# Residual x plus attention moved from VectorE in the attention steps to GpSimd in the dense layer (one core)

## The chip, the cores and the metric

One NeuronCore of a Trainium2 chip runs the whole program in one launch. The metric is device time in microseconds; the figure for the kernel before is the median of three runs. The granted TensorE clock is 0.99 of full speed on average in the profiled execution.

## The reference

Input x and context ctx are both (8, 512, 2048). Per batch and per channel, a correlation over the 512 positions picks 12 shifts, and a weighted sum of shifted context rows is the attention output. A layer norm, a dense layer with eight small gated experts, and a second residual follow.

```python
def _autocorrelation(Q, K, V):            # called with layernorm(x), ctx, ctx
    corr = ifft(fft(q) * conj(fft(k))).real
    w, idx = top_k(corr, 12); w = softmax(w)
    out = sum(w[i] * take_along_axis(v, min(idx[i] + pos, L - 1)))
x = x + tanh(g_xattn[0]) * _autocorrelation(_layernorm(x), ctx, ctx)
base = layernorm(x) @ W_base.T + b_base
gate = softmax(xf @ W_gate.T); thr = sigmoid(xf @ W_thr + b_thr) * 0.125
w = relu(gate - thr) / sum; moe = einsum(h, w, B_w) * 2.0
x = x + tanh(g_ffn[0]) * (base + moe)
```

## The kernel before

**Attention.** 32 steps, one for each batch and chunk of 512 channels (`STEPS`). Transforms are matmuls against tables. Every engine runs its own `step(i, par, phase)`, with the front of chunk i and the back of chunk i-1 in one step. TensorE does `q_spectra(i)` (L422), `turn_w(i-1)` (transposes, L435), `w_spectra(i-1)` (L454, L460), `correlate(i)` (L472), `v_spectra(i+1)` and `out_tiles(i-1)` (L488), which leaves in PSUM, for each half h of a mirrored pair, a cosine part and a sine part. The eight PSUM banks are two sets of four, `X(par)`; `turn_w` may write the banks of a half only once its output has been taken out.

A row of a chunk's output and its mirror image are cosine plus sine and cosine minus sine. VectorE's `residual` (L758, L764), last in its step, forms both: it adds gate times cosine to x rows, then plus or minus gate times sine, in `xres_mem`. SyncE (the DMA queue SP) brings x in for it with ten DMAs per step (`load_res`, L308 and L311) and writes the sum with ten (`store`, L318 and L321) to the scratch `x2`. The x rows lie in mirrored order, so eight of each ten DMAs cover 16 partitions. GpSimd does the folds and the sums of products; its `fold_v` (L834) waits for VectorE's `w_made`.

**Weights.** Then `turn_weights` transposes 20 jobs through PSUM (L1070): `b_w`, sixteen row blocks of `w_base`, `a_w`, the gate and the first normalised row tile. ScalarE takes out the high half (`weights_hi`, L1138) and VectorE the low half (`weights_lo`, L1194). The first four rows of `w_base` are loaded in the last attention steps (`early_weights`), the others by L999 as slots come free.

**Dense layer.** 32 row tiles of 128 rows. For tile i TensorE does `base(i)`, 192 matmuls (L1097), `turn_hw(i)` (L1105), `logits(i+1)` and `experts(i)`, 12 matmuls (L1112 to L1114). ScalarE's step is `gating(i)`, `normalise(i+2)`, `rounded(i+2)` (L1156), `hw_hi(i)` (L1175); VectorE's is `gating(i)`, `statistics(i+2)` (L1202), `hw_lo(i)` (L1249), `finish(i)` (L1256). `experts(i)` waits for `hw_hi(i)` and `hw_lo(i)`, so these stand behind the normalising of tile i+2 in both queues. GpSimd adds the bias to the residual row (L1285) and makes the f16 remainder of the normalised tile (L1281). SyncE issues, in a step: two transposing DMAs of tile i+1 (L1026), the load of tile i+2 into `norm` (L1018), the load of residual row i+1 into one of two `row` buffers (L1032), the store of row i (L1043).

## Time and profile before

| | us |
|---|---|
| median of 3 runs (lowest, highest) | 3028.21 (3028.15, 3030.24) |
| the profiled execution: its own time | 3031.29 |
| its span in the trace | 3029.5 |
| TensorE matmul busy | 2921.9 (96%) |
| VectorE busy | 1606.0 (53%) |
| ScalarE busy | 1012.6 (33%) |
| GpSimd busy | 1454.0 (48%) |
| attention: to the last output matmul | 0 to 1441.8 |
| weights: to the first dense matmul | 1441.8 to 1507.3 |
| dense layer: 32 tiles | 1507.3 to 3029.5 |

Busy shares over the whole span mix the two long stages, of which each has its own limits: VectorE and GpSimd are nearly full in the first and nearly idle in the second. TensorE is nearly full in both.

### The profile page before, as it was taken

The numbers are of one execution on the slowest core, as the hardware profiler recorded it, in microseconds if no ns is written. First come the engines' busy times: TensorE is split into PE (matmuls) and PEld (weight loads), VectorE is DVE, ScalarE is ACT, GpSimd is POOL, SyncE is SP. The second block draws the span as 40 slices with busy tenths as digits, with TensorE's granted clock in tenths as the row PEclk, the third lists the DMA queues.
The fourth block names the chain that finished last, engine by engine and source line by source line (L and its number), as shares of the span: only waits on it lengthen the run. The fifth ranks groups of instructions, "written<-read, shape, count | busy, mean of one in ns | idle before, by whom it ended". The sixth has DMA issues, their size and how long they took to land.

```text
span 3029.5 us, 37059 instructions
## 1 busy us (share of the span) xinstructions
PE 2921.9 (96%) x13184; PEld 1466.0 (48%) x13184; DVE 1606.0 (53%) x2738; ACT 1012.6 (33%) x1672; POOL 1454.0 (48%) x577
## 2 busy tenths in 40 slices
PE   4999999999999999997799999999999999999999
PEld 2445554555545554553644444444444444444444
DVE  3899989999999999998722121121211112111111
ACT  4555556555555545441511121111211112111110
POOL 4788888889888888884031211212112121221210
PEclk8999999999999999999899999999999999999999
DMA  8455544555455554423634132331323313233230
GB/s 201 124 123 126 139 110 118 127 132 125 115 122 125 135 117 102 101 73 111 237 98 111 56 111 75 91 111 55 111 72 94 106 60 111 69 97 99 68 97 28
DMA packets 260355, 324.49 MB, mean 107 GB/s; under 512 B 162911, under 2 KB 163487, under 8 KB 245541
## 3 DMA queue, kind: packets, MB, share of 16 engines
q1 hardware_dynamic: 259922, 323.38, 40.1%
q8 instruction: 29, 0.48, 0.1%
q14 instruction: 56, 0.46, 0.0%
q10 hardware_dynamic: 348, 0.18, 0.0%
HBM read 223.76 MB, written 67.21 MB: 96 GB/s over the span
## 4 chain that ended last, share of the span: by engine, by line
PE 84%; DVE 5%; POOL 3%; issue 2%; DMA 2%; ACT 1%; SPq 1%; ACTq 0%; DVEq 0%; POOLq 0%
PE bank L1097 43%; PE bank L488 7%; PE bank L422 7%; PE bank L454 6%; PE bank L472 5%; PE bank L460 3%; POOL spec_o L869 3%; DVE rows_mem L1256 2%; PE bank L1086 1%; PE bank L1087 1%; PE bank L1088 1%; ACT wt L548 1%; PE bank L435 1%; PE bank L405 1%; PE bank L411 1%
## 5 line engine op out<-in xcount | busy, mean ns | idle before, releaser
L1281 POOL TENSOR_TENSOR rows_mem<-norm,rows_mem 128x2048 f16<-128x2048 f32 x31 | 126.1, 4068 | 1220.7 <-ACT rows_mem L1156 1220.7
L1097 PE MATMUL bank<-w_hi,rows_mem 128*128 128x512 f16 x2048 | 489.3, 379 | 3.8 <-DVE rows_mem L1256 3.8
L1097 PE MATMUL bank<-w_hi,xres_mem 128*128 128x512 f16 x2048 | 489.0, 379 | 3.5 <-DVE rows_mem L1256 3.5
L869 POOL TENSOR_TENSOR spec_o<-spec_o,term 128x1024 f32<-128x1024 f32 x190 | 443.3, 2362 | 40.6 <-DVE term L686 40.6
L1249 DVE TENSOR_TENSOR hwt_lo<-bank,hwt_hi 128x128 f16<-128x128 f32 x32 | 9.3, 292 | 790.4 <-ACT hwt_hi L1175 790.4
L1097 PEld LDWEIGHTS bank<-w_hi,rows_mem 128*128 128x128 f16 x2048 | 200.2, 98 | 251.6 <-DVE rows_mem L1256 13.6
L1097 PEld LDWEIGHTS bank<-w_hi,xres_mem 128*128 128x128 f16 x2048 | 200.2, 98 | 250.6 <-DVE rows_mem L1256 12.7
L488 PE MATMUL bank<-spec_o,table 128*128 128x512 f32 x512 | 249.1, 617 | 19.9 <-POOL spec_o L869 15.8
L1097 PE MATMUL bank<-w_lo,xres_mem 128*128 128x512 f16 x1024 | 262.8, 379 | 0.0
L1097 PE MATMUL bank<-w_lo,rows_mem 128*128 128x512 f16 x1024 | 262.8, 379 | 0.0
L422 PE MATMUL bank<-rows_mem,table 128*128 128x512 f32 x512 | 227.7, 598 | 18.0 <-POOL rows_mem L849 15.7
L454 PE MATMUL bank<-wt,table 128*128 128x512 f16 x1024 | 232.7, 379 | 8.3 <-ACT wt L548 8.3
L472 PE MATMUL bank<-table,prod_a 128*128 128x256 f32 x1024 | 231.5, 385 | 7.2 <-POOL prod_a L855 7.2
L1202 DVE BATCH_NORM_STATS2 stats<-norm 128x6 f32<-128x512 f32 x128 | 79.1, 681 | 299.4 <-DMA norm<-x_scratch 299.4
L1175 ACT ACTIVATE hwt_hi<-bank 128x128 f16<-128x128 f32 x32 | 8.9, 277 | 657.4 <-PE bank L1105 657.4
L472 PEld LDWEIGHTS bank<-table,prod_a 128*128 128x128 f32 x1024 | 193.7, 192 | 43.2 <-POOL prod_a L855 8.0
L422 PEld LDWEIGHTS bank<-rows_mem,table 128*128 128x128 f32 x512 | 98.1, 192 | 142.7 <-issue 142.7
L454 PEld LDWEIGHTS bank<-wt,table 128*128 128x128 f16 x1024 | 97.0, 98 | 130.5 <-ACT wt L548 12.3
L1285 POOL TENSOR_TENSOR rows_mem<-rows_mem,b_rows 128x2048 f32<-128x2048 f32 x32 | 144.1, 4503 | 30.6 <-DMA rows_mem<-x_scratch 30.6
L1097 PEld LDWEIGHTS bank<-w_lo,xres_mem 128*128 128x128 f16 x1024 | 100.2, 98 | 119.1
L1097 PEld LDWEIGHTS bank<-w_lo,rows_mem 128*128 128x128 f16 x1024 | 100.1, 98 | 119.0
L488 PEld LDWEIGHTS bank<-spec_o,table 128*128 128x128 f32 x512 | 92.2, 192 | 130.3 <-issue 102.6
(182 smaller groups left out, 4876.3 us busy)
## 6 DMA issues: line engine op xcount, KB each, us to landing
rows_mem<-in_x_dram SPq DMA_DIRECT2D x32, 1024.0 KB, 13.0
norm<-x_scratch SPq DMA_DIRECT2D x32, 1024.0 KB, 5.5
rows_mem<-x_scratch SPq DMA_DIRECT2D x32, 1024.0 KB, 7.0
out_dram<-rows_mem SPq DMA_DIRECT2D x32, 1024.0 KB, 4.4
norm<-in_x_dram SPq DMA_DIRECT2D x28, 1024.0 KB, 10.8
rows_mem<-in_ctx_dram SPq DMA_DIRECT2D x256, 64.0 KB
rows_mem<-in_ctx_dram SPq DMA_DIRECT2D x64, 256.0 KB
xres_mem<-in_x_dram SPq DMA_DIRECT2D x256, 64.0 KB
```

What stands on the lines that cost most here:

```text
L405: pe.matmul(imag[:, 0, :], v_tab[:, EI, :], v_sym[:, 3, :], start=True, stop=True)
L422: mm = pe.matmul(pair(four, half)[:, row, :], q_tab[:, 2 * half + row, j, :], qf[:, 2 * row + j, :], start=(j == 0), stop=(j == 1))
L454: pe.matmul(pair(to, half)[:, row, :], w_tab[:, h, 2 * half + row, j, :], wt16[:, 0, 2 * y + j, :], start=(j == 0 and h == 0), stop=False)
L460: mm = pe.matmul(pair(to, half)[:, row, :], w_tab[:, 0, 2 * half + row, j, :], wt16[:, 1, 2 * y + j, :], start=False, stop=(j == 1))
L472: mm = pe.matmul(four[:, ct, row * HALF:(row + 1) * HALF], prod_a[:, slot, ct * 128:(ct + 1) * 128], p_tab[:, slot, :], start=(half == 0), ...
L488: mm = pe.matmul(to[:, part, :], o_tab[:, slot, :], spec_o[:, h, slot, :], start=(row == 0), stop=(part == 1 and row == 1))
L869: pool.tensor_tensor(to, to, buffer, sign).then_inc(term_added, 1)
L1097: mm = pe.matmul(dense[o][:, :], nt(par, part)[:, k, :], w[:, k, o * 512:(o + 1) * 512], start=(k == 0 and n == 0), stop=False)
L1202: op = dve.bn_stats(stats[:, q, :], norm[:, q * C:(q + 1) * C])
L1256: dve.scalar_tensor_tensor(out=row[:, par, cols], in0=dense[o][:, :], scalar=out_gate[:, :], in1=row[:, par, cols], op0=ALU.mult, op1=ALU. ...
L1281: pool.tensor_tensor(norm_lo, norm[:, :], norm_hi, ALU.subtract).then_inc(norm_lo_made, 1)
L1285: pool.tensor_tensor(row[:, par, :], row[:, par, :], bias[:, :], ALU.add).then_inc(bias_added, 1)
```

## The change

In the attention steps ScalarE copies both parts of each half, times the gate, out of PSUM into one buffer `kept` (`keep_out`), and one DMA stores them as they are in a scratch `part_scratch`. No x is loaded for it and nothing is added there. In the dense layer a row tile is now the `after` rows (even tiles) or the `before` rows (odd tiles) of a half, so that cosine and sine parts have one layout for both. For each tile the x rows go into `norm` (eight DMAs of 16 partitions for even tiles, one reversed one for odd ones), the cosine part into `addend`, GpSimd adds it, the sine part goes into the same `addend`, GpSimd adds or subtracts it, and the sum is written to `x2_rows` and read again later as the residual row. `row` is one buffer now, since `addend` takes the other. Tile 0 is formed in the attention stage, in the last step but one and the last.

```diff
+    x2_rows = nc.dram_tensor("x2_scratch", (ROWS, 128, D), f32, kind="Internal").ap()
+    parts = nc.dram_tensor("part_scratch", (2 * B, 2, 128, D), f32, kind="Internal").ap()
...
+                def store(i):
+                    sp.wait_ge(out_kept, 2 * (i + 1))
+                    sp.dma_start(parts[2 * b:2 * b + 2, :, :, c:c + C].rearrange("h a p c -> p (h a) c"),
+                                 kept.rearrange("p h a c -> p (h a) c")).then_inc(parts_stored, 16)
...
+                def first_tile():
+                    sp.wait_ge(xstat_used, STEPS - NCH)
+                    sp.wait_ge(parts_stored, 16 * NCH)
+                    for n in range(8):
+                        sp.dma_start(norm[16 * n:16 * n + 16, :], x_half[0, 1, 7 - n]).then_inc(first_loaded, 16)
...
-                            pe.wait_ge(sine_added, 4 * (c - 1) + 2 * (y + 1))
+                            pe.wait_ge(out_kept, 2 * (c - 1) + y + 1)
...
+                def keep_out(c, four, h):
+                    if h == 1 and least(c) >= 1:
+                        act.wait_ge(parts_stored, 16 * c)
+                    act.wait_ge(out_made, 2 * c + 2 - h)
+                    act.activation(kept[:, h, :, :], pair(four, 1 - h), ACT.Copy, scale=gates[:, 0:1]).then_inc(out_kept, 1)
...
+                    if least(i) >= 1:
+                        keep_out(i - 1, mine, 1)
                     if most(i) < STEPS:
                         scale_w(i)
+                    if least(i) >= 1:
+                        keep_out(i - 1, mine, 0)
...
-                    if least(i) >= 1:
-                        residual(i - 1, 1 - par, mine)
...
                 def load(i, par):
-                    if fleast(i) >= 2:
-                        sp.wait_ge(out_stored[par], 16 * (i // 2))
+                    if fleast(i) >= 1:
+                        sp.wait_ge(out_stored[1 - par], (128, 16)[1 - par] * ((i - 1) // 2 + 1))
+                    sp.wait_ge(x2_kept, 16 * (i + 1))
...
                 def step(i, par):
+                    if fmost(i) + 2 < ROWS:
+                        load_norm(i + 2, par)
                     if fmost(i) + 1 < ROWS:
                         turn(i + 1, 1 - par)
                     if fmost(i) + 2 < ROWS:
-                        load_norm(i + 2)
+                        load_sine(i + 2)
+                        keep_x2(i + 2)
...
             def statistics(dve, i):
-                dve.wait_ge(norm_loaded, 16 * (i + 1))
+                dve.wait_ge(formed, 2 * (i + 1))
...
+                def form(i, par):
+                    pool.wait_ge(norm_loaded[par], (144 * (i // 2), 32 * (i // 2 + 1))[par])
+                    pool.tensor_tensor(norm[:, :], norm[:, :], addend, ALU.add).then_inc(formed, 1)
+                    pool.wait_ge(sine_loaded, 16 * i)
+                    pool.tensor_tensor(norm[:, :], norm[:, :], addend, (ALU.add, ALU.subtract)[par]).then_inc(formed, 1)
...
                 def step(i, par):
...
                     if fmost(i) + 2 < ROWS:
+                        form(i + 2, par)
                         remainder(i + 2, par)
```

The DMA queue (SP) in the middle of the dense layer, two tiles, before: transposes, next tile, residual row, store.

```order
L1026 DMA_TRANSPOSE xres_mem<-rows_mem 128x16x128 x2
L1018 DMA norm<-x_scratch 128x2048
L1032 DMA rows_mem<-x_scratch 128x2048
L1043 DMA out_dram<-rows_mem 128x2048
L1026 DMA_TRANSPOSE rows_mem<-rows_mem 128x16x128 x2
L1018 DMA norm<-x_scratch 128x2048
L1032 DMA rows_mem<-x_scratch 128x2048
L1043 DMA out_dram<-rows_mem 128x2048
```

And the same queue in the changed kernel, from the store of an even tile on:

```order
L1053 DMA out_dram<-rows_mem 16x2048 x8
L1039 DMA rows_mem<-x_scratch 128x2048
L1013 DMA norm<-in_x_dram 128x1x2048
L1014 DMA rows_mem<-part_scratch 128x2048
L1032 DMA_TRANSPOSE parts_mem<-rows_mem 128x16x128 x2
L1019 DMA rows_mem<-part_scratch 128x2048
L1024 DMA x_scratch<-norm 128x2048
L1055 DMA out_dram<-rows_mem 8x16x2048
L1039 DMA rows_mem<-x_scratch 128x2048
L1011 DMA norm<-in_x_dram 16x2048 x8
L1014 DMA rows_mem<-part_scratch 128x2048
```

The store of a row now stands ahead of the load of the next residual row; cosine part, sine part and the write of the sum are new, and the load into `norm` stands ahead of the transposes.

GpSimd at the start of the dense layer, before:

```order
L1281 TENSOR_TENSOR rows_mem<-norm,rows_mem 128x2048
L1285 TENSOR_TENSOR rows_mem<-rows_mem,b_rows 128x2048
L1281 TENSOR_TENSOR rows_mem<-norm,rows_mem 128x2048
L1285 TENSOR_TENSOR rows_mem<-rows_mem,b_rows 128x2048
L1281 TENSOR_TENSOR rows_mem<-norm,rows_mem 128x2048
```

And in the changed kernel (L1302 and L1304 are the two adds, L1298 the remainder, L1308 the bias):

```order
L1302 TENSOR_TENSOR norm<-norm,rows_mem 128x2048
L1304 TENSOR_TENSOR norm<-norm,rows_mem 128x2048
L1298 TENSOR_TENSOR rows_mem<-norm,rows_mem 128x2048
L1308 TENSOR_TENSOR rows_mem<-rows_mem,b_rows 128x2048
L1302 TENSOR_TENSOR norm<-norm,rows_mem 128x2048
L1304 TENSOR_TENSOR norm<-norm,rows_mem 128x2048
L1298 TENSOR_TENSOR rows_mem<-norm,rows_mem 128x2048
```

The two adds of a tile stand behind the bias of the tile two before it, and ahead of its own remainder.

ScalarE where attention ends, before (L1138 takes out the first weights):

```order
L568 ACTIVATE corr_mem<-corr_mem,w_inv 128x512 x4
L548 ACTIVATE wt<-bank 128x1024 x2
L1138 ACTIVATE corr_mem<-bank 128x1024 x2
L1143 ACT_TABLE_LOAD
L1143 ACTIVATE std<-var 128x1
```

And in the changed kernel:

```order
L565 ACTIVATE parts_mem<-bank,gates 128x1024
L558 ACTIVATE corr_mem<-corr_mem,w_inv 128x512 x4
L565 ACTIVATE parts_mem<-bank,gates 128x1024
L538 ACTIVATE wt<-bank 128x1024 x2
L565 ACTIVATE parts_mem<-bank,gates 128x1024 x2
L1154 ACTIVATE corr_mem<-bank 128x1024 x2
L1159 ACT_TABLE_LOAD
L1159 ACTIVATE std<-var 128x1
```

The copies of the last chunk's output now stand ahead of the first weights and of the square root.

## Rows read from the trace of the kernel before

**Rows 1.** Windows: stretch, its us, busy us of each engine, clock, DMA share, GB/s.

```profile
510.87:680.96 170.09, 168.99 (x597) 86.00 (x597) 156.50 (x218) 93.14 (x173) 149.31 (x64) 1.00 0.52 124
...
2124.97:2172.44 47.47, 47.24 (x254) 22.92 (x254) 8.87 (x30) 7.92 (x10) 8.53 (x2) 1.00 0.29 88
```

**Rows 2.** Timeline of one attention step: start, us, engine, line, operation, idle before and releaser.

```profile
722.48 2.56 ACT L568 ACTIVATE corr_mem<-corr_mem,w_inv 128x512 f32<-128x512 f32 x4 [1.79 <-DVE w_inv L749]
722.50 2.68 DVE L758 SCALAR_TENSOR_TENSOR xres_mem<-bank,gates,xres_mem 128x1024 f32<-128x1024 f32 x2
...
727.08 0.74 DVE L764 SCALAR_TENSOR_TENSOR xres_mem<-bank,gate_neg,xres_mem 128x512 f32<-128x512 f32 x1
...
727.89 3.61 SPq L318 DMA_DIRECT2D x_scratch<-xres_mem  x8
...
730.57 1.91 PE L435 MATMUL bank<-ident,corr_mem 128*128 128x128 f32 x16
```

**Rows 3.** Timeline, end of a step in which a new batch's scales are made.

```profile
719.65 0.30 PEld L488 LDWEIGHTS bank<-spec_o,table 128*128 128x128 f32 x2 [0.91 <-POOL spec_o L869]
```

**Rows 4.** Timeline, GpSimd in the second attention step.

```profile
84.97 2.37 POOL L834 TENSOR_TENSOR rows_mem<-rows_mem 128x1024 f32<-128x1024 f32 x1 [20.49 <-DMA rows_mem<-in_ctx_dram]
```

**Rows 5.** Timeline where attention ends and the weights are turned.

```profile
1407.88 1.09 PE L435 MATMUL bank<-ident,corr_mem 128*128 128x128 f32 x8 [2.70 <-DVE xres_mem L764]
...
1437.03 1.94 ACT L1138 ACTIVATE corr_mem<-bank 128x1024 f16<-128x1024 f32 x2 [25.68 <-PE bank L1070]
...
1439.83 1.98 PE L488 MATMUL bank<-spec_o,table 128*128 128x512 f32 x4
...
1441.56 2.35 DVE L1194 SCALAR_TENSOR_TENSOR corr_mem<-bank,corr_mem 128x1024 f16<-128x1024 f32 x2
...
1449.07 8.08 PE L1070 MATMUL bank<-ident,rows_mem 128*128 128x128 f32 x48 [4.01 <-DVE xres_mem L764]
...
1455.16 28.83 SPq L999 DMA_DIRECT2D rows_mem<-in_L_ffn_W_base_dram  x12
...
1463.02 12.19 PE L1070 MATMUL bank<-ident,rows_mem 128*128 128x128 f32 x80 [5.87 <-DMA rows_mem<-in_L_ffn_W_base_dram]
```

**Rows 6.** Timeline, the load of tile 1 at the start of the dense layer.

```profile
1500.52 0.35 SPq L1018 DMA_DIRECT2D norm<-x_scratch  x1
```

**Rows 7.** The chain that ended last: start, us, what (first dense tile).

```profile
1507.29 41.44 PE bank L1097 x192
```

**Rows 8.** Timeline of one dense tile, which begins at 2124.97.

```profile
2121.34 0.38 PE L1112 MATMUL bank<-corr_mem,hwt_hi 128*128 128x512 f16 x1
...
2125.43 6.73 SPq L1026 DMA_TRANSPOSE xres_mem<-rows_mem  x2
...
2132.26 0.77 SPq L1018 DMA_DIRECT2D norm<-x_scratch  x1
...
2137.78 2.47 DVE L1202 BATCH_NORM_STATS2 stats<-norm 128x6 f32<-128x512 f32 x4 [9.90 <-DMA norm<-x_scratch]
...
2144.54 1.91 ACT L1156 ACTIVATE rows_mem<-norm 128x2048 f16<-128x2048 f32 x1
...
2146.65 4.07 POOL L1281 TENSOR_TENSOR rows_mem<-norm,rows_mem 128x2048 f16<-128x2048 f32 x1 [38.70 <-ACT rows_mem L1156]
...
2150.68 4.51 POOL L1285 TENSOR_TENSOR rows_mem<-rows_mem,b_rows 128x2048 f32<-128x2048 f32 x1
...
2166.14 0.28 ACT L1175 ACTIVATE hwt_hi<-bank 128x128 f16<-128x128 f32 x1 [19.69 <-PE bank L1105]
```

**Rows 9.** Windows of 1 us: 128-partition loads, then stores in 16-partition pieces.

```profile
2136.00:2137.00 1.00, 1.00 (x6) 0.48 (x5) 0.00 (x0) 0.00 (x0) 0.00 (x0) 1.00 1.07 451
...
1411.00:1412.00 1.00, 1.00 (x6) 0.49 (x5) 1.00 (x2) 0.35 (x1) 0.00 (x0) 1.00 0.83 139
```

**Rows 10.** After a long TensorE idle: its first matmuls (timeline), the clock (windows).

```profile
43.08 9.66 PE L422 MATMUL bank<-rows_mem,table 128*128 128x512 f32 x16 [15.67 <-POOL rows_mem L849]
...
47.00:49.00 2.00, 2.00 (x4) 0.72 (x3) 0.00 (x0) 1.97 (x8) 1.92 (x2) 0.69 0.16 60
```

More of the change, by code:

```diff
@@ L877, in gpsimd_attention, with first_tile @@
                 fold_v(1)
+                def first_tile():
+                    pool.wait_ge(first_loaded, 160)
+                    pool.tensor_tensor(norm[:, :], norm[:, :], parts_mem[:, D:2 * D], ALU.add).then_inc(formed, 1)
+                    pool.wait_ge(formed, 1)
+                    pool.tensor_tensor(norm[:, :], norm[:, :], rows_mem[:, 0, :], ALU.add).then_inc(formed, 1)
                 def step(i, par, phase):
+                    if most(i) == STEPS - 1:
+                        pool.wait_ge(w_made, 4 * i)
+                        first_tile()
                     if least(i) >= 1 and most(i) + 1 < STEPS:
@@ L936, in weight_row @@
             def weight_row(n):
-                m = n - 1
-                return (row if m % 4 < 2 else wrow)[:, m % 2, :]
+                return rows_mem[:, (n - 1) % 4, :]
             def weight_target(n, h, part):
@@ L1255, in finish @@
                         dve.wait_ge(dense_made, 4 * i + o + 1)
-                        dve.scalar_tensor_tensor(out=row[:, par, cols], in0=dense[o][:, :], scalar=out_gate[:, :],
-                                                 in1=row[:, par, cols], op0=ALU.mult, op1=ALU.add).then_inc(out_ready, 1)
+                        dve.scalar_tensor_tensor(out=row[:, cols], in0=dense[o][:, :], scalar=out_gate[:, :],
+                                                 in1=row[:, cols], op0=ALU.mult, op1=ALU.add).then_inc(out_ready, 1)
                 def step(i, par):
```

132 lines of the change are left out of this document (58 added, 74 removed).

## The prediction

> **What bounds the kernel now.** I read the windows of the two long stages first. In four attention steps TensorE is busy 168.99 of 170.09 us, in one dense tile 47.24 of 47.47 [rows 1]: each stage runs at TensorE's pace, 42.5 us per step and 47.47 per tile, so the 156 us of VectorE work in four steps costs nothing as long as it ends before TensorE asks for it. Then I read the timeline of a step for what VectorE's residual holds up, of the seams (prologue, end of attention, weights, first tile) for TensorE's waits, and of one dense tile for how late each result of the side chain is against its need. The change has TensorE do the same matmuls. It can win only what TensorE waits for VectorE's residual or for DMAs that stood behind it in a queue, and it loses wherever the longer chain of the dense layer comes later than TensorE's need.
>
> **Attention steps, all but the last.** Removed: from 722.50 to 727.82 VectorE forms the residual [rows 2], about 5.3 us a step, and 19 of the 20 residual DMAs (eight of them take SP 3.61 us to issue [rows 2]). Added: two ScalarE copies of 128x1024 out of PSUM, about 1 us each (L1138 takes 1.94 for two [rows 5]). The first falls in ScalarE's idle of 1.79 us ahead of `scale_w`, the second follows it at 725.04 and ends at about 726.1; TensorE's transposes, which now wait for these copies, begin at 730.57 [rows 2]. The cover is 4.4 us; without it a late copy would cost TensorE its lateness one for one. Nothing ends earlier for it: VectorE's next product waits for the spectra that TensorE makes, and in the one step of four where TensorE waits for anything at the end (0.91 us of idle in weight loads, of which some 0.24 stand in every gap [rows 3]), it waits for GpSimd, whose chain starts from `w_made` and the new scales, which stand ahead of the residual on VectorE before and after. So 0 for these steps, with 0.1 us per step lost to 0.1 gained as bounds, 3 us in all. In the second step GpSimd's `fold_v` starts at 84.97, after a DMA of v that stood behind the first residual loads [rows 4]; `w_made`, its other wait, comes about a microsecond earlier. Gain 1.
>
> **Last step and weights.** TensorE waits 2.70 us for the residual ahead of its transposes [rows 5]. The changed wait is for copies that are ready, so 2.7 is won. At the end TensorE's second weight job waits 4.01 us more for the last residual [rows 5]. That goes too, but a new wait takes its place. `keep_out` of the last half needs the last output matmuls, which end at 1441.81 (1439.83 and 1.98), and the first `weights_hi`, which ran at 1437.03, stands behind it on ScalarE, with the square root and so VectorE's low parts (L1194, 1441.56, 2.35 for two) behind that. In the old frame less 2.7: matmuls end 1439.1, copy to 1440.2, high parts to 1442.1, square root with its table load and VectorE's short chain to about 1445, low parts to 1447.4, TensorE's job 1 done at 1448.4, against 1449.07 for the start of job 2 before. By TensorE alone the gain would shrink to 0.7. But the next stop is the DMA of the fifth block of `w_base`: it was issued at 1455.16, since ten stores of the residual stood ahead of it on SP, and TensorE waited 5.87 us for it, to 1463.02 [rows 5]. Now one store stands there and the load goes out when job 1 is turned, at about 1448.5; with the same 7.9 us to its use, TensorE goes on at 1456.4. From there each job waits for one megabyte every 2.5 us, about what the DMA engines carry (451 GB/s [rows 9]), so the lead lasts. Gain 6.6 in all at the first dense tile, between 0.7 and 8.
>
> **Start of the dense layer.** The chain of a tile is now serial. Durations: a megabyte of 128 partitions takes 5.5 us from issue (2132.26) to first use (2137.78); from there to the end of the rounding takes 8.67 (2144.54 + 1.91); a remainder 4.07; an add of 128x2048 f32 4.51; SP issues the two transposes in 6.73 [rows 8]. The load of tile 1 goes out at 1500.52 [rows 6], when all weights are turned. Then: x and cosine part, two loads at once, 7.9 us (a second megabyte adds about 2.4 at 451 GB/s [rows 9]); add 4.5; sine part 5.5, which cannot be fetched sooner because it uses the same buffer; add 4.5; to rounding 8.7; remainder 4.1: 1535.7. Only then may tile 2 be loaded: eight x DMAs and the part take 4 us to issue and 5.5 to land; add 4.5, sine 5.5, add 4.5, to rounding 8.7: 1568.4. `hw_hi(0)` and `hw_lo(0)`, 0.3 each, stand behind this on ScalarE and VectorE, and `experts(0)` waits for both. TensorE is ready for `experts(0)` at 1507.29 [rows 7] plus 43.84 (2121.34 is 3.63 ahead of the tile border at 2124.97, and a tile has 47.47 [rows 1, 8]), so at 1551.1. Before, the chain was done long before that. After, TensorE idles to about 1568.9: **17.5 us lost once**. Bounds: 14, if four waits land 0.8 sooner, and 22, if the eight-piece loads go at the rate of [rows 9].
>
> After an idle of 15.67 us the clock granted to TensorE was still 0.69 on average from 47 to 49, after matmuls that began at 43.08 [rows 10]: some 5 us at the lower level (1.2 GHz), which costs 2.6 us. I add 2.5, from 0 to 3.
>
> **Steady tiles.** The `row` buffer is single, so a new ring runs through a tile. Put the border (2124.97 above) at 0, for an odd tile. Store of the even tile's row in eight pieces: 3.6 us to issue, landed at 6 to 9.5, I take 7.5. Residual row: 13.0. Bias on GpSimd: 17.5. Behind the row come x and cosine part, landed at 18.2; add to 22.7. The transposes, issued behind them, hold the DMA engines for some 7 us, to about 25; sine part 28.2; add 32.7; rounding done 41.4; `hw_hi` and `hw_lo` 42.0. The need is at 43.84. So **1.8 us of cover**; for an even tile (one store, landed at 5.6; part landed by 17) the rounding is done at 40.2, cover 3. `statistics(i+2)`, which now waits for the sum, has `hw_lo(i)` and `finish(i)` behind it on VectorE, and `normalise(i+2)` has `hw_hi(i)` behind it on ScalarE: that is the whole path. ScalarE's wait for the write of the sum is covered, since that lands while the statistics and the square root run. The remainder ends at 45.5, ahead of the next bias. DMA load rises from 29% of the tile [rows 1] by three megabytes at 2.4 us, 7.2 of 47.5, to 44%. So 0 per tile, and I count 0.
>
> **Sum.** Against the profiled execution's own 3031.29 us: -1 -6.6 +17.5 +2.5 = +12.4, 3043.7. The median of the runs is 3.1 lower than that execution, which gives 3040.6; I say 3040, some 0.4% slower.
>
> **Rivals.**
> *R1, the ring binds.* One thing could make it: DMAs on 16 partitions. In a window of such stores the engines moved 139 GB/s at a share of 0.83, against 451 for whole tiles [rows 9]. By that rate the eight-piece store takes 7.5 us (landed at 9.5, two later than I took) and the eight x pieces as much where I took 4. That uses up 2 us of 1.8. If the larger queue also makes the row, part and sine loads land 1 us later each, an odd tile is 3 over and an even one as much, and the ring pays it in each of 30 tiles: +90. If only the odd ones are 2 over, +30, 3070. Against it: those windows had rows of 2 KB and were paced by SP's issue (64 KB per 0.45 us), and the pieces here have rows of 8 KB. I price R1 at 3070. The Trainium skill ("SBUF — State Buffer", Door 1: The DMA port swizzle) speaks against this change here: 16 neighbouring partitions reach only four of the sixteen ports, a quarter of the bandwidth. By it a store in eight pieces would take some 10 us and land at about 12; the odd tiles would be some 3 us over, and the sum would be about 3087, an estimate from that page. The trace leans that way with its third of the full rate, but doesn't separate ports from issue.
>
> *R2, not slower.* TensorE's stall at the first tile is offset in the weights. If the jobs were held by late issue and not by the DMA rate, then with SP free they would run at VectorE's pace of 2.35 us per job (two of L1194 [rows 5]) instead of about 2.8 (1463.02 to the first dense work near 1503 for 14 jobs); 14 jobs win 6, and with the loads at their fastest the stall is 14. Sum: -1 -12.6 +14 +2.5 = +3: 3031. It decides from the moment a block of `w_base` lies ready when TensorE comes for it. Against: the engines were already full there.
>
> *R3, faster.* VectorE's free time ends GpSimd's chain sooner, and TensorE's waits in attention (0.67 us in seven steps) go as well, on top of R2: below 3022. I see no link by which it would.
>
> **How the numbers follow.** Forecast (3031 to 3050) 0.62; R1 (above 3050) 0.20; R2 (3024 to 3034) 0.14; R3 0.04. A measurement of this kernel can tell about 0.2%, 6 us, so "same" is 3022 to 3034: R2 and a sliver of the forecast, 0.16. Slower 0.80, faster 0.04. The range, 3030 to 3075, leaves out most of R3, part of R2 and the upper half of R1.
>
> **What would show it.** In the profile after: attention steps of 42.5 us with no wait of L425 for `keep_out`; the fifth `w_base` load some 6 us earlier; one wait of TensorE of about 17 us at the first `experts` for `hwt_lo` or `hwt_hi`, with the clock down after it; dense tiles still of 47.47. Tiles of 48 or more with a TensorE wait at `experts` in every one, or every second one, mean R1; a residual row that lands later than 15 us after the border would say so first. The forecast is wrong low if the first stall is under 8 us, and wrong high if any per-tile wait stands.

## The result, and the profile after

The changed kernel takes 3259.98 us, the median of four runs (3248.72 to 3267.11), against 3028.36 (3028.15 to 3030.24) beside it: a ratio of 1.076, 95% interval 1.0727 to 1.0793. The prediction said 3040, at most 3075. The sign was right and the size was not: 232 us are lost where 12 were forecast.

The profiled execution of the changed kernel took 3256.94 us (span 3255.1). Its page shows where TensorE is less busy. The rows are busy tenths in 40 slices of 81 us.

```profile
PE 2992.7 (92%) x13184; PEld 1483.0 (46%) x13184; DVE 1454.1 (45%) x2546; ACT 1071.1 (33%) x1735; POOL 1742.6 (54%) x641
...
PE   4999999999999999977798989898989898989898
```

Attention, the first 17 slices, stays full. Slices 18 to 20 (7) are the weights and the first tile. After them TensorE alternates between 9 and 8: it loses time in the dense tiles one after another. The windows view gives the attention stage by itself (columns as in [rows 1]):

```profile
127.00:1365.00 1238.00, 1229.07 (x4336) 626.41 (x4335) 991.85 (x1406) 712.36 (x1240) 1087.02 (x465) 1.00 0.30 96
```

TensorE is busy 99.3% of it, as in [rows 1]. Its waits, summed over the span (who waited, for what, us in total, times, the longest):

```profile
PE bank L1128 <- DVE hwt_lo L1266: 147.8, 31, 13.6
...
PE bank L1102 <- DMA rows_mem<-rows_mem: 11.4, 1, 11.4
...
PE bank L1121 <- DVE hw L1257: 1.4, 1, 1.4
...
PE bank L425 <- ACT parts_mem L565: 0.3, 1, 0.3
```

L1128 is `experts`. It waits for `hwt_lo` in 31 tiles: 13.6 us in tile 0, 3.6 to 6.5 us in the next 29 (133.4 together), and 0.9 once more, as in the kernel before. L425, the transposes that now wait for ScalarE's copies, wait 0.3 us in the whole program.

**The books.** VectorE's four residual products mark the end of a tile. Their first start, in tile 0 and in the last tile, of the kernel before (L1256) and then of the changed one (L1273), in the timeline:

```profile
1552.53 2.07 DVE L1256 SCALAR_TENSOR_TENSOR rows_mem<-bank,out_gate,rows_mem 128x512 f32<-128x512 f32 x3 [3.05 <-PE bank L1114]
...
3022.34 2.73 DVE L1256 SCALAR_TENSOR_TENSOR rows_mem<-bank,out_gate,rows_mem 128x512 f32<-128x512 f32 x4 [1.06 <-PE bank L1114]
```

```profile
1571.52 0.75 DVE L1273 SCALAR_TENSOR_TENSOR rows_mem<-bank,out_gate,rows_mem 128x512 f32<-128x512 f32 x1 [1.70 <-PE bank L1130]
...
3242.61 2.73 DVE L1273 SCALAR_TENSOR_TENSOR rows_mem<-bank,out_gate,rows_mem 128x512 f32<-128x512 f32 x4 [1.06 <-PE bank L1130]
```

Up to tile 0's first product: +19.0 us. From there to the last tile: 1671.1 against 1469.8, +201.3, in tiles of 54.2 us on average instead of 47.5 (the last, of 45.7 in both, left out). From there to the end of the span: 12.5 against 7.2 (spans 3255.1 and 3029.5), +5.3. Together +225.6, the whole difference of the spans. The prediction had +12.4 in the first of these terms, 0 in the second, and did not name the third.

**One tile of 54.9 us.** SP's, GpSimd's and the experts' rows of the timeline, from the border at 2007.81 (the store of an even tile) to the next at 2062.70. `rows_mem` is both `row` and `addend`; L1308 adds the bias, L1302 the cosine part, L1304 the sine part.

```profile
2007.81 4.19 SPq L1053 DMA_DIRECT2D out_dram<-rows_mem  x8
2014.66 0.34 SPq L1039 DMA_DIRECT2D rows_mem<-x_scratch  x1
2015.11 0.66 SPq L1013 DMA_DIRECT2D norm<-in_x_dram  x1
2015.83 0.45 SPq L1014 DMA_DIRECT2D rows_mem<-part_scratch  x1
2016.37 18.60 SPq L1032 DMA_TRANSPOSE parts_mem<-rows_mem  x2
2020.12 4.51 POOL L1308 TENSOR_TENSOR rows_mem<-rows_mem,b_rows 128x2048 f32<-128x2048 f32 x1 [13.93 <-DMA rows_mem<-x_scratch]
2033.20 4.50 POOL L1302 TENSOR_TENSOR norm<-norm,rows_mem 128x2048 f32<-128x2048 f32 x1 [8.57 <-DMA rows_mem<-part_scratch]
2037.78 0.33 SPq L1019 DMA_DIRECT2D rows_mem<-part_scratch  x1
2042.55 4.50 POOL L1304 TENSOR_TENSOR norm<-norm,rows_mem 128x2048 f32<-128x2048 f32 x1 [4.84 <-DMA rows_mem<-part_scratch]
...
2054.00 1.91 ACT L1173 ACTIVATE rows_mem<-norm 128x2048 f16<-128x2048 f32 x1
2055.82 0.26 ACT L1192 ACTIVATE hwt_hi<-bank 128x128 f16<-128x128 f32 x1
2056.18 0.29 DVE L1266 TENSOR_TENSOR hwt_lo<-bank,hwt_hi 128x128 f16<-128x128 f32 x1 [4.54 <-ACT hwt_hi L1192]
...
2056.62 0.58 PE L1128 MATMUL bank<-corr_mem,hwt_hi 128*128 128x512 f16 x1 [4.82 <-DVE hwt_lo L1266]
...
2062.70 0.67 SPq L1055 DMA_DIRECT2D out_dram<-rows_mem  x1
2072.01 0.32 SPq L1039 DMA_DIRECT2D rows_mem<-x_scratch  x1
2072.43 3.71 SPq L1011 DMA_DIRECT2D norm<-in_x_dram  x8
...
2087.07 4.50 POOL L1302 TENSOR_TENSOR norm<-norm,rows_mem 128x2048 f32<-128x2048 f32 x1 [5.08 <-DMA rows_mem<-part_scratch]
```

The chain is the one of the prediction: store, row, x and cosine part, sine part, norm, rounding (L1173), and behind it on ScalarE and VectorE the two small products of the tile before, for which TensorE has waited 4.82 us. What is late are x and the cosine part. In this tile the reversed x load goes out at 2015.11 and GpSimd can add at 2033.20: 18.1 us. In the next the store is the reversed one: the residual row, which waits for its end, goes out 9.3 us after it (2062.70 to 2072.01), and x in eight pieces takes 14.6 (2072.43 to 2087.07). Counted from the border, as in the prediction: the store of eight pieces ends where I put it (row out at 6.9; I had 7.5), but x and the cosine part are used at 25.4 instead of 18.2, and the rounding ends at 48.1 instead of 41.4, where 43.84 is the need. In the next tile the cosine part is used at 24.4 instead of 17: 3.7 of that is the reversed store (9.3 instead of 5.6), and as much the eight pieces of x.

**The clock.** Windows of 2 us around the same wait; the last three numbers of a row are granted clock, DMA share, GB/s.

```profile
2050.00:2052.00 2.00, 1.79 (x30) 1.61 (x27) 1.11 (x7) 0.44 (x2) 0.00 (x0) 1.00 0.16 66
2052.00:2054.00 2.00, 0.00 (x0) 0.00 (x0) 0.00 (x0) 1.85 (x1) 0.00 (x0) 1.00 0.00 0
2054.00:2056.00 2.00, 0.00 (x0) 0.00 (x0) 0.00 (x0) 2.00 (x3) 0.00 (x0) 0.70 0.00 0
2056.00:2058.00 2.00, 1.38 (x4) 0.58 (x5) 0.29 (x1) 1.53 (x3) 1.93 (x1) 0.50 0.00 0
2058.00:2060.00 2.00, 2.00 (x7) 0.60 (x5) 1.38 (x2) 0.00 (x0) 2.00 (x1) 0.50 0.00 0
2060.00:2062.00 2.00, 2.00 (x7) 0.77 (x6) 1.00 (x3) 0.00 (x0) 0.13 (x1) 0.59 0.00 0
```

While TensorE waits, its clock falls from 2.4 to 1.2 GHz, and it comes back at about 2061.6, five us after work has begun again. Of 201.3 us, 133.4 are the waits. The other 68, some 2.3 a tile, go with these stretches at half clock: after each of the 29 waits windows of 1 us show the lower level for another 2.8 to 6 us of work, 133 us in all, and half of that, 66.5, is what the lower level costs.

### The profile page after: what moved, and what is told of

It reads as the page before. It is cut to its first block, busy times and chain, and to the rows that moved or that the text cites. A ratio compares the mean times of both kernels' runs of the same rounds, so it can differ in the third digit from the quotient of the medians.

```text
span 3255.1 us, 36779 instructions
## 1 busy us (share of the span) xinstructions
PE 2992.7 (92%) x13184; PEld 1483.0 (46%) x13184; DVE 1454.1 (45%) x2546; ACT 1071.1 (33%) x1735; POOL 1742.6 (54%) x641
## 4 chain that ended last, share of the span: by engine, by line
PE 37%; issue 25%; POOL 18%; DMA 7%; DVE 6%; ACT 5%; SPq 0%; POOLq 0%; ACTq 0%; DVEq 0%
PE bank L478 6%; PE bank L412 6%; PE bank L444 6%; DMA rows_mem<-part_scratch 6%; PE bank L462 5%; POOL norm L1302 4%; POOL norm L1304 4%; POOL rows_mem L1308 4%; PE bank L450 3%; POOL spec_o L852 3%; PE bank L1113 3%; POOL rows_mem L1298 2%; ACT norm L1162 2%; DVE stats L1219 2%; ACT rows_mem L1173 2%
## 5 line engine op out<-in xcount | busy, mean ns | idle before, releaser
L1113 PE MATMUL bank<-w_hi,parts_mem 128*128 128x512 f16 x2048 | 489.5, 379 | 2.7 <-DVE rows_mem L1273 2.5
L1308 POOL TENSOR_TENSOR rows_mem<-rows_mem,b_rows 128x2048 f32<-128x2048 f32 x32 | 144.2, 4505 | 515.0 <-DMA rows_mem<-x_scratch 515.0
L1113 PEld LDWEIGHTS bank<-w_hi,parts_mem 128*128 128x128 f16 x2048 | 200.9, 98 | 252.3 <-DVE rows_mem L1273 12.2
L1302 POOL TENSOR_TENSOR norm<-norm,rows_mem 128x2048 f32<-128x2048 f32 x31 | 139.7, 4505 | 294.6 <-DMA rows_mem<-part_scratch 294.6
L1298 POOL TENSOR_TENSOR rows_mem<-norm,rows_mem 128x2048 f16<-128x2048 f32 x31 | 125.9, 4062 | 280.0 <-ACT rows_mem L1173 280.0
L1113 PE MATMUL bank<-w_lo,parts_mem 128*128 128x512 f16 x1024 | 262.8, 379 | 0.0
L1304 POOL TENSOR_TENSOR norm<-norm,rows_mem 128x2048 f32<-128x2048 f32 x31 | 139.6, 4502 | 153.3 <-DMA rows_mem<-part_scratch 153.3
L1128 PE MATMUL bank<-corr_mem,hwt_hi 128*128 128x512 f16 x128 | 74.0, 578 | 147.8 <-DVE hwt_lo L1266 147.8
L1113 PEld LDWEIGHTS bank<-w_lo,parts_mem 128*128 128x128 f16 x1024 | 100.2, 98 | 119.1
```

The costliest lines, as they stand in the source:

```text
L1113: mm = pe.matmul(dense[o][:, :], nt(par, part)[:, k, :], w[:, k, o * 512:(o + 1) * 512], start=(k == 0 and n == 0), stop=False)
L1298: pool.tensor_tensor(norm_lo, norm[:, :], norm_hi, ALU.subtract).then_inc(norm_lo_made, 1)
L1302: pool.tensor_tensor(norm[:, :], norm[:, :], addend, ALU.add).then_inc(formed, 1)
L1304: pool.tensor_tensor(norm[:, :], norm[:, :], addend, (ALU.add, ALU.subtract)[par]).then_inc(formed, 1)
L1308: pool.tensor_tensor(row, row, bias[:, :], ALU.add).then_inc(bias_added, 1)
```

## Experiments

Three theories are told apart (C's part on `hw_hi` and `hw_lo` came only with the later runs). **A**: the x loads and output stores in mirrored order (eight DMAs of 16 partitions, or one reversed one) are slow in themselves. **B**: the larger queue is what is slow (three more megabytes a tile, and transposes behind them). **C**: whatever is slow does harm only through the order of work: the single `row` buffer and the norm of the tile two ahead, which stand ahead of `hw_hi` and `hw_lo`.

| run | us, median | ratio to before | tiles after tile 0 |
|---|---|---|---|
| straight loads and stores | 3037.81 | 1.0023 (1.0013 to 1.0033) | 47.5 |
| straight loads | 3044.19 | 1.0047 (1.0031 to 1.0064) | 47.5 |
| straight stores | 3106.95 | 1.0248 (1.0229 to 1.0267) | 47.5 to 53.5 |
| loads ahead of the store | 3056.88 | 1.0085 (1.0068 to 1.0101) | 47.5 |
| nothing formed | 3021.10 | 0.9969 (0.9957 to 0.9981) | 47.5 |
| `hw_hi`, `hw_lo` first | 3041.00 | 1.0040 (1.0025 to 1.0055) | 47.5 |
| that, and first transposes first | 3039.22 | 1.0031 (1.0019 to 1.0043) | 59.9, then 47.5 |
| that, all transposes first | 3026.74 | 0.9994 (0.9985 to 1.0003) | 47.5 |
| two column halves | 3227.87 | 1.0641 (1.0624 to 1.0659) | 53.8 |
| pieces of 32, reversed in 64 | 3276.45 | one run | 60.5 and 48.7 by turns |
| pieces of 64, eight groups | 3038.39 | one run | 47.5 |

The kernel before took 3029.9 to 3031.4 in these sessions.

### Straight loads and stores

```diff
-                    if par == 0:
-                        for n in range(8):
-                            sp.dma_start(norm[16 * n:16 * n + 16, :], x_half[i // 2, 1, 7 - n]).then_inc(norm_loaded[0], 16)
-                    else:
-                        sp.dma_start(norm[:, :], x_half[i // 2, 0, :, ::-1, :]).then_inc(norm_loaded[1], 16)
+                    sp.dma_start(norm[:, :], x_straight[i]).then_inc(norm_loaded[par], 16)
```

and the stores likewise, to `out_straight[i]`.

> The x rows of a dense tile are loaded, and the finished rows stored, straight, in one DMA over 128 partitions each; the mirror order is left out, so rows meet the wrong parts. All else is the changed kernel, its ring and its seven megabytes per tile too. Theory A (DMAs on 16 partitions or in reversed order are slow: 17.3 us from issue to the first add for x and cosine part of an odd tile, 9.3 us for the reversed store): loads of about 8 us and stores of about 5 take over 7 us out of the ring of each tile, more than the 4.8 us that TensorE waits, so the waits at the experts and the slow clock behind them go in all tiles but the first ones: 3030 to 3060 us. Theory B (the queue as such: three more megabytes, transposes in the same queue): the waits stay, 3180 us or more.

Measured: 3037.81. 222 us of the loss are gone at the same number of bytes, and some 6.5 are left against the kernel before of the same session (3031.36). The same stretch of a tile in this run:

```profile
2036.69 0.34 SPq L1049 DMA_DIRECT2D out_dram<-rows_mem  x1
2040.60 0.32 SPq L1037 DMA_DIRECT2D rows_mem<-x_scratch  x1
2041.03 0.37 SPq L1011 DMA_DIRECT2D norm<-in_x_dram  x1
...
2051.50 4.51 POOL L1296 TENSOR_TENSOR norm<-norm,rows_mem 128x2048 f32<-128x2048 f32 x1 [1.43 <-DMA rows_mem<-part_scratch]
```

The row follows the store after 3.9 us, and x and cosine part are there 10.5 after issue, though the queue carries the same megabytes and the transposes behind them. A stands. B falls as the cause of the loss, though a larger queue isn't free: the two transposes keep SP some 11 us here, and 6.73 in [rows 8]. `experts` waits 14.8 us in tile 0 and 0.9 in one other.

### Loads alone, stores alone

The two halves of the edit above, one in each run.

> Only the loads of x rows are straight and single; the stores are as in the changed kernel. Mirror order of the loads is left out. Theory A: an odd tile's ring is some 9 us shorter and its wait gone, an even tile's 3 us shorter and 2 us of its 4.8 left: 3045 to 3100 us. Theory B: over 3200 us.

> Only the stores of finished rows are straight and single; the loads are as in the changed kernel. Mirror order of the stores is left out. Theory A: the ring behind a reversed store is 4.8 us shorter, that behind an eight-piece store 2.4: waits of about 0 and 2.4 us are left: 3090 to 3160 us, more than with straight loads. Theory B: over 3200 us.

Measured: 3044.19 with straight loads, 1 us under its range, and 3106.95 with straight stores, within it. With straight loads the reversed store still takes 9.3 us (2085.53 to the row at 2094.81) and the tiles are 47.5 all the same: the cover holds it. With straight stores x and cosine part of an odd tile come 18.6 us after issue, of an even one 15.3, and 18 waits at `experts` sum to 52.1 us. So the slow loads break the cover by themselves, by 2.0 us a tile on average (tile 0 to the last: 1528.8 against 1469.8), the slow stores alone do not, and both together cost 6.7: what cover takes up is free, and only the rest is paid. The spans of the first two runs are 6.7 us apart, in two places: 5.3 at the very end, where the last store is the reversed one (the last tile's products start at 3030.35 of a span of 3042.8, against 3028.98 of 3036.1 with straight stores: 12.4 and 7.1 to the end), and 1.4 before it.

### Another order on SP and GpSimd

The slow transfers stay; x and parts of the next tile but one are issued ahead of the store of the last row, and GpSimd forms ahead of the bias.

```diff
                 def step(i, par):
                     if fmost(i) + 2 < ROWS:
                         load_norm(i + 2, par)
+                    if fleast(i) >= 1:
+                        store_row(i - 1, 1 - par)
                     if fmost(i) + 1 < ROWS:
                         turn(i + 1, 1 - par)
                     if fmost(i) + 2 < ROWS:
                         load_sine(i + 2)
-                        keep_x2(i + 2)
...
+                    load(i, par)
+                    if fmost(i) + 2 < ROWS:
+                        keep_x2(i + 2)
```

> Same work and result as the changed kernel, other order: the load of x and cosine part goes out ahead of the store of the finished row, the load of the residual row behind that of the sine part, and GpSimd forms the sum ahead of the bias. So the store and the residual row leave the ring of the sum. Theory C (the ring through the single row buffer is what makes the slow DMAs cost): rounding done some 38 us after the tile border instead of 48, no wait at the experts: 3030 to 3070 us. If the sum's own chain (slow loads, two adds, sine) binds without the ring: over 3150 us.

Measured: 3056.88; every tile after the second is 47.5 long, with the slow transfers in it. The harm came through the order (C). Tile 0 ends 14.8 us later than in the straight run (1572.63 and 1557.81): 10.5 of it is TensorE's wait for the second tile's transposes, issued behind the third tile's slow load, which the straight run does not have; it was 2.2 behind at the first dense matmul already (1499.01 and 1496.82), and the rest fits the clock behind the longer waits. The end costs the 5.3 again.

### The attention half alone

The attention and weights of the changed kernel, the dense layer of the one before, on straight x; nothing is formed (tiles 1 and up lack the attention output).

> The changed attention and weights, with the dense layer of before: straight loads and stores of x, two row buffers, no stored part added by GpSimd (from the second tile on the attention output is left out of x, so the output is not the reference's; the work of the matmuls is the same). It measures by itself what the copies out of PSUM give before the dense layer. By the trace of the changed kernel (first dense matmul near 1495.5 instead of 1507.29) this half is worth 11 to 12 us: 0.4% below the kernel before, ratio 0.9955 to 0.9970. By the prediction's own terms (1 and 6.6, and nothing for the first-tile stall) it would be 7.6 us, ratio 0.9975. By the rival that the lead is given back in the first dense tiles, because the load of tile 1 starts at the end of the weights as before, the ratio is 0.999 to 1.000.

Measured: 0.9969, which is 9.4 us (5.8 to 13.0) faster than before. Both the 11 to 12 expected from the trace of the changed kernel and the 7.6 of the prediction lie within that interval, so the run does not choose between them; its own trace is 8.1 ahead at tile 0 and at the end. The rival that the lead is given back in the first tiles lies outside. The first half of the change is worth what it was meant to be worth.

### The experts' own products first

```diff
                 def step(i, par):                      # ScalarE
+                    hw_hi(i)
                     if fmost(i) + 2 < ROWS:
                         normalise(i + 2)
-                    hw_hi(i)
...
                 def step(i, par):                      # VectorE
...
+                    hw_lo(i)
+                    finish(i, par)
                     if fmost(i) + 2 < ROWS:
                         statistics(dve, i + 2)
-                    hw_lo(i)
-                    finish(i, par)
```

> The changed kernel with hw_hi ahead of normalise on ScalarE and hw_lo and finish ahead of statistics on VectorE, and nothing else. Against the run with the transposes first as well it prices the wait for the second tile's transposes. Theory A+C: TensorE's waits at the experts go in all tiles, one wait of about 11 us for the transposes of the second tile stays, with its slower clock behind it: 3030 to 3038, ratio 1.000 to 1.003, 11 to 14 above the run with the transposes first. If the chain of the norm is longer than a tile by itself, 3060 to 3190.

> The changed kernel with three orders changed: hw_hi ahead of normalise on ScalarE, hw_lo and finish ahead of statistics on VectorE, so that TensorE's experts wait for the tile's own products alone and not for the norm of the tile two ahead; and the two transposes of the second tile issued ahead of the third tile's loads on SP. The slow loads and stores stay. Theory A+C (slow transfers are harmful only because the chain runs into hw_hi and hw_lo of the tile before): the steady tiles go back to about 47.5, the wait of 11.4 for the transposes goes, and what stays is the gain before the dense layer of 11 to 12: 3017 to 3025, ratio 0.996 to 0.999. If the remaining chain of norm, remainder and transposes of the tile ahead is itself longer than a tile (it takes some 54 us now, part of which was TensorE's own lateness), tiles stay at 48 to 52 and the time is 3050 to 3180. If the queue's transfers disturb TensorE by themselves (rival B), tiles are over 48 with no wait of TensorE at the experts.

Measured: 3041.00, 3 us above its range, with the one wait of 11.0 for the second tile's transposes that it left in, and 3039.22 with the second tile's transposes ahead of the third tile's loads. The steady tiles went back to 47.5 in both, as C said, with the slow transfers still there. So the 201 us needed both: slow transfers, and small products that stand behind the norm of a later tile; to take away either is enough. But the second run gained only 1.8 on the first, not 11 to 14, and missed its range by 14. Its wait had moved by one tile:

```profile
1575.76 0.68 SPq L1013 DMA_DIRECT2D norm<-in_x_dram  x1
1576.49 0.45 SPq L1014 DMA_DIRECT2D rows_mem<-part_scratch  x1
1577.04 16.55 SPq L1032 DMA_TRANSPOSE parts_mem<-rows_mem  x2
...
1596.06 0.27 PE L1104 MATMUL bank<-parts_mem 128*128 128x137 f16 x1 [9.84 <-DMA parts_mem<-rows_mem]
```

The third tile's transposes stand behind the reversed load of the fourth, and SP needs 16.55 us to issue the two, where it needs 6.73 in [rows 8].

### All transposes first

```diff
                 def step(i, par):                      # SP
-                    if fmost(i) + 2 < ROWS:
-                        load_norm(i + 2, par)
                     if fmost(i) + 1 < ROWS:
                         turn(i + 1, 1 - par)
                     if fmost(i) + 2 < ROWS:
+                        load_norm(i + 2, par)
+                    if fmost(i) + 2 < ROWS:
                         load_sine(i + 2)
                         keep_x2(i + 2)
```

beside the edit to ScalarE and VectorE above.

> The changed kernel with hw_hi, hw_lo and finish ahead of the next norm, and the transposes of the next tile always issued ahead of the loads of the tile after it (the run e7 did so for the second tile only). The slow loads and stores stay. In e7 TensorE waits 9.8 us for the third tile's transposes, issued at 1577 behind a reversed load and 16.6 us long. Ahead of the load they are issued at about 1576 and take 6 to 7: done near 1584, before TensorE's need at about 1586. Then no stall of over 2 us is left, the clock stays up, all tiles are 47.5, and the lead of some 10 us from before the dense layer stays: e7 less 12 to 15: ratio 0.9955 to 0.9985 of the kernel before, 3018 to 3027. Rival: the loads that now go out 7 us later make the norm of tile 3 late, and the wait moves one tile on: 5 to 10 us once, ratio 1.000 to 1.003. Rival: the ring through the row buffer binds with the later loads: tiles over 48, 3060 or more.

Measured: 3026.74, a ratio of 0.9994, 12.5 us below the run before it. The time is at the upper end of the expected 3018 to 3027, the ratio above the expected 0.9955 to 0.9985. From the first dense tile on no wait of TensorE is over 1.5 us, and tile 0 is ahead of the kernel before by 10.8 (1552.53 there):

```profile
1541.71 2.73 DVE L1273 SCALAR_TENSOR_TENSOR rows_mem<-bank,out_gate,rows_mem 128x512 f32<-128x512 f32 x4 [3.05 <-PE bank L1130]
...
3011.53 2.73 DVE L1273 SCALAR_TENSOR_TENSOR rows_mem<-bank,out_gate,rows_mem 128x512 f32<-128x512 f32 x4 [1.06 <-PE bank L1130]
```

The lead of 10.8 us holds to the last tile. The span is only 5.5 shorter (3024.0 against 3029.5), since 5.3 go to the reversed last store; the medians are 3.2 apart. Part of the 10.8 may be luck of that one trace (see the attention steps, in the part on the prediction). The whole change, in this order, can't be told from the kernel before, and is 233 us better than in the order that it came in. No version that computes the whole was measurably faster than before.

### What makes these transfers slow

Three runs change the form of the x loads. In the first and the third the stores are straight and rows of x come to other places.

```diff
+                        for n in range(4):           # even tiles: 4 pieces of 32
+                            sp.dma_start(norm[32 * n:32 * n + 32, :], x_straight[i, 32 * n:32 * n + 32, :])...
+                        sp.dma_start(norm[:, :], x_grp[i, :, ::-1, :])...     # odd: 2 groups of 64 reversed
```

> The changed kernel with straight stores, and with loads of x in other shapes: even tiles in four pieces of 32 partitions in their straight order, odd tiles in one DMA whose rows are reversed within each 64 instead of each 16 (rows of x come to other places, so the output is not the reference's; bytes are the same). It asks what makes these loads slow. If the number of neighbouring partitions of one DMA sets its rate (ports), four pieces of 32 move about twice the 139 to 156 GB/s of eight pieces of 16 while they are alone in the queue: 250 to 320 GB/s, x and part landed 7 to 8.5 us after issue instead of 10.9. If SP's issue of pieces sets it, about the same, since four pieces take half the time to issue, but the rate then falls once the last is issued. If pieces as such are slow whatever their width, still 10 or more. For the reversed load: if the descending order of rows makes it slow, 17 us for x and part as before; if it is that the DMA is cut into eight groups of 16 rows, groups of 64 make it much faster or slower than 17. Time between 3045 and 3110, by the waits at the experts.

```diff
-                        sp.dma_start(norm[:, :], x_half[i // 2, 0, :, ::-1, :]).then_inc(norm_loaded[1], 16)
+                        for n in range(2):
+                            cols = slice(n * D // 2, (n + 1) * D // 2)
+                            sp.dma_start(norm[:, cols], x_half[i // 2, 0, :, ::-1, cols]).then_inc(norm_loaded[1], 16)
```

> The changed kernel with the reversed x load as two DMAs of half the columns each, nothing else: same bytes, twice the descriptors of half the size. Theory G, if the two DMAs are given different engines: share of the engines near 1.0 instead of 0.5, landing of x and part 11 to 12 us instead of 17.3, odd waits at the experts gone, tiles of about 50 to 52: 3130 to 3200. Theory G, if both use the same eight engines: no change, 17 to 18 us and 3240 to 3270. If the cost is in the descriptors and not in the engines, slower: 20 us or more and above 3280.

```diff
+                        for n in range(2):           # even tiles: 2 pieces of 64
+                            sp.dma_start(norm[64 * n:64 * n + 64, :], x_straight[i, 64 * n:64 * n + 64, :])...
+                        sp.dma_start(norm[:, :], x_half[i // 2, 0])...        # odd: 8 groups of 16, ascending
```

> The changed kernel with straight stores, even x loads in two pieces of 64 partitions in straight order, and odd x loads in the changed kernel's shape of 8 groups of 16 rows, but ascending within each group (rows of x come to other places, so the output is not the reference's; bytes are the same). The run before this one had groups of 64 reversed: after the first megabytes the engines moved 52 GB/s at a share of 0.12 of the sixteen, two engines' worth for two groups, where eight groups give 126 to 140 at 0.5, eight engines' worth. Theory G: the number of groups of such a load is the number of engines that carry it. If the compiler merges the ascending groups into one straight load, x and part land 10 to 11 us after issue and the descending order is what forces the groups; if they stay apart, 16 to 18 us as in the changed kernel, and order plays no part. Pieces of 64: 16 partitions move 148 GB/s and 32 about 210 at a full share. If the partitions limit it (ports), 64 are at or above 300 GB/s and x and part land within 11 us; if only the number of pieces did, the same.

The end of the program shows one reversed store with nothing beside it. First the kernel before (straight), then the changed kernel: window, us, clock, mean busy share of the 16 engines, GB/s.

```profile
3026.00:3028.00 2.00, 1.00 1.04 426
```

```profile
3247.00:3249.00 2.00, 1.00 0.48 98
3249.00:3251.00 2.00, 0.62 0.48 147
3251.00:3253.00 2.00, 0.50 0.50 193
```

A share of 0.48 to 0.50 is what eight busy engines of sixteen would show; a mean alone could also be sixteen engines that are busy half of the time. The load with two groups of 64, in the first of the three runs:

```profile
2036.00:2039.00 3.00, 1.00 0.12 52
2039.00:2042.00 3.00, 1.00 0.12 52
```

0.12 is two of sixteen, and x and cosine part come 28.3 us after issue; this run took 3276.45, where I expected 3045 to 3110. Reversal is in both loads; what differs is 8 groups against 2, and the share follows it, 0.5 against 0.12. Ascending groups came 10.5 us after issue, at 348 to 426 GB/s, like a straight load. In that run TensorE's tiles are 47.5 again. So the slow load needs the reversed order as well as the groups. That ascending groups were joined into one straight load, and that reversed order matters by keeping them apart, would fit both runs; no run shows it. The Trainium skill ("DMA: Bandwidth & Descriptors", Why a DMA increments its semaphore by 16 and not by 1) has the rule: a DMA is spread over the largest number of engines, at most 16, that divides the slowest dimension of both sides. By it 8 groups give 8 engines and 2 give 2, and the traces agree.

Two halves by columns took 3227.87, between the two cases that I had set: the share stays near 0.5 (150 GB/s at 2024 to 2026), x and cosine part come after 16.9 us instead of 18.1, and tiles are 53.8. That fits two DMAs on the same eight engines and not on all sixteen.

Pieces of fewer partitions, in the windows where the piece loads are alone: eight of 16 (the changed kernel), four of 32, two of 64.

```profile
2080.00:2082.00 2.00, 1.00 0.98 143
2082.00:2084.00 2.00, 1.00 0.98 148
```

```profile
2094.00:2096.00 2.00, 1.00 1.05 221
2096.00:2098.00 2.00, 1.00 0.86 197
```

```profile
2095.00:2097.00 2.00, 1.00 1.04 221
```

The engines are busy nearly the whole time (0.86 to 1.05), at a third or half of the 426 GB/s of a whole tile; so it is not SP's issue that paces them, which the prediction left open. 64 partitions are no faster than 32, against what I expected of that run. The Trainium skill ("SBUF — State Buffer", Door 1: The DMA port swizzle) says both: 16 partitions reach four of the sixteen ports, and 32 and 64 reach the same eight. The trace agrees with the second, and gives 143 to 148 for the first, above the quarter of the page.

## Why the prediction was wrong, point by point

**Attention steps, 0: right.** The waits for `out_kept` sum to 0.3 us, the busy share of the stage is unchanged. The 1 us of the second step can't be checked on one trace: of the twelve traces with this attention half, five gain 0.6 to 0.7 us there and seven 2.2 to 2.7. When the last `q_spectra` begins (1357.86, against 1361.17 before), the changed kernel is 3.3 us ahead. The twelve traces have 0.6 to 4.6, the most in the run with all transposes first. There is one trace of the kernel before, so this can't be split into gain and scatter.

**Last step and weights, -6.6: right, a little too small.** The transposes of the last step wait 0.3 us instead of 2.70. The predicted new wait (high parts behind `keep_out`) is there; TensorE's first large weight job starts at 1442.12 after 6.93 us of it:

```profile
1442.12 16.69 PE L1086 MATMUL bank<-ident,rows_mem 128*128 128x128 f32 x112 [6.93 <-DVE corr_mem L1211]
...
1445.80 26.30 SPq L990 DMA_DIRECT2D rows_mem<-in_L_ffn_W_base_dram  x12
```

The fifth `w_base` load goes out 9.4 us earlier than in [rows 5], and I had 6.7; tile 1's load at 1488.99 is 11.5 earlier than in [rows 6]. But 3.3 of both is the lead from the attention steps. Between there and the first dense matmul (1495.98, against 1507.12) the changed kernel wins 7.8, and the twelve traces 7.0 to 8.8. The low parts end at 1443.1, 7.9 us after the last output matmul (1435.19); I had 8.3 (1447.4 and 1439.1). TensorE waits only for the first of the two.

**First tile, +17.5 and +2.5: right in place, too small.** (The working gives 1568.9 less 1551.1, which is 17.8.) TensorE lost 30.4 us from its first logits matmul to the end of tile 0 (19.0, and the lead of 11.4 that it had, 1491.45 against 1502.89): 13.6 at the experts, 11.4 ahead of them for the second tile's transposes, which I had not put behind the third tile's loads in this sum, 1.4 for `hw`, and some 4 by the clock. The straight run has 14.8 at the experts and nothing of the 11.4, so my bounds, 14 to 22, held for fast transfers.

**Steady tiles, 0: wrong, and this is the 201 us.** The step that failed is the line "Behind the row come x and cosine part, landed at 18.2". It priced the reversed load as a whole tile, and the reversed store likewise: 7.2 us too little in odd tiles, 7.4 in even ones (3.7 the store, 3.7 the eight pieces), against a cover of 1.8 and 3. That leaves 5.4 and 4.4; the measured waits are 5.2 us on average in odd tiles and 4.0 in even ones. I had put the 139 GB/s at 0.83 of the engines [rows 9] down to SP's pace, against R1; but the 143 to 148 here, at 0.98, are the rate of such pieces with the engines full.

**R1 had the ring right, half of the cause, and the wrong price.** It named the ring, 16 partitions and a wait at the experts in every tile, and was given 3070 by taking only the odd tiles, 2 us each; even its worst case of +90 lacked the reversed DMAs and the clock. The store that it feared in odd tiles was in time (row out at 6.9, where R1 had 9.5 or more); what was late there is the reversed load, which it did not name. Only the eight pieces of x in even tiles were slow as it said. A tile's lateness was 4.6 us of wait on average and some 2.3 of half clock, and odd and even tiles both paid it.

**The end of the program: not named, +5.3.** Nothing covers the last store in any of these runs.

**R2 and R3** needed the first-tile stall to be small. R2's mechanism did not come. Its 2.8 us per weight job took in the end of the stage: before, the jobs already followed each other every 2.5 us (1484.16, 1486.65), each behind a wait of 0.5 for its block, and they do so after:

```profile
1461.50 1.97 PE L1086 MATMUL bank<-ident,rows_mem 128*128 128x128 f32 x16 [0.43 <-DMA rows_mem<-in_L_ffn_W_base_dram]
1463.99 1.97 PE L1086 MATMUL bank<-ident,rows_mem 128*128 128x128 f32 x16 [0.52 <-DMA rows_mem<-in_L_ffn_W_base_dram]
```

With all transposes first the time is within R2's 3024 to 3034 by another way: the stall of the first tile goes altogether, and the last store takes 5.3 of the lead.

## What to carry to other kernels

Price a DMA by its form before its bytes: read the slowest dimension on each side as the instruction has it, and the number of partitions of each piece. A product that TensorE waits for in this tile should not stand, on its engine, behind the work for a tile further on; a queue that is only 2 us early is no cover, and a short wait costs its clock as well. And look at the last transfer of the program: here its form cost 5.3 us in full.

## What the runs showed of the hardware

- A DMA of 1 MB cut into 8 groups of 16 reversed rows shows a busy share of 0.48 to 0.50 of the DMA engines, at 98 to 193 GB/s; one of 2 groups of 64 reversed rows a share of 0.12, at 52. A straight one moved 426. Why the first half of the reversed store is slower (98) than the last (193) at the same share is open.
- Pieces of 16 partitions move 143 to 148 GB/s with all engines busy; pieces of 32 move 197 to 221, of 64 221 (one run each).
- Waits of TensorE of 3.6 to 6.5 us were each followed by 2.8 to 6 us of work at 1.2 GHz: some 67 us over 29 tiles beside 133 of waiting. In the run with one wait of 9.84 us, its tile was 12.4 longer, 2.6 of that from the clock.
- Two DMA transposes of 128x2048 take SP 6.73 us [rows 8], some 11 behind a straight load and the cosine part, 15.8 to 19.7 behind a reversed one (steady tiles), and some 29 behind the load of two groups; the size is the same in all.
